# One mixture-of-experts phase: VectorE's side work spread one piece to a chunk, two router exponentials made from Tanh and squares, later down products

## The chip, the cores and the metric

One core of one Trainium2 chip runs the kernel. The metric is device time in microseconds (us) of one execution. The engines are named as in the profile: PE is TensorE, ACT is ScalarE, DVE is VectorE, POOL is GpSimd, SP is SyncE.

## What is computed

A small language-model tower over x, 8 sequences of 256 tokens: a stack of causal convolutions with a log-softmax, a linear attention, and a transformer block whose second half is the part of interest. With 2048 rows of 64 channels, 8 experts and top 2:

```
flat = rmsnorm(x, ln2_w)                       # 2048 x 64
probs = softmax(flat @ router_w.T)             # 2048 x 8
tp, ti = top_k(probs, 2);  tp = tp / (sum(tp) + 1e-09)
weights = sum over the two of tp * one_hot(ti)
for e in range(8):                             # hidden size 170
    hh = silu(flat @ w1[e].T) * (flat @ w3[e].T)
    out = out + weights[:, e:e+1] * (hh @ w2[e].T)
return x + out
```

## The kernel before

Each engine has its own program, written out by hand; the order of the work is the order in these programs, and semaphores join them. The change touches the last phase, the experts, and the router work that stands among them.

The 2048 rows are four pairs (n_ = 0 to 3) of 512 rows. For each pair the 8 experts are 11 chunks (i = 0 to 10): 8 chunks are the first 128 hidden units of an expert, and 3 chunks (the 1st, 5th and 9th in the order) are the remaining 42 units of three experts together. So there are 44 chunks, numbered u = 11 * n_ + i. What happens to chunk u:

- PE multiplies by w1 (two matmuls of 512 columns, a high and a low half of the weights) into one of two banks, then by w3 into one of two others (lines 1949 to 1959). The w1 product waits until ACT has done the silu of chunk u - 2, the w3 product until DVE has read chunk u - 2.
- ACT makes the silu of the w1 product (line 825), then the 16-bit cast, the high part, of chunk u - 1 (line 810).
- DVE multiplies the silu by the w3 product into a ring of 6 buffers (line 1362). This is called the product of chunk u below.
- POOL subtracts the high part to get the low part (line 414, `low_part`).
- When the parts of two experts are there, PE makes their down products (`down(n_, k, t_)`, k = 0 to 3 the two experts 2k and 2k + 1, t_ = 0 to 3 a block of 128 rows). `FILLED = (3, 6, 8, 11)` says how many chunks of the pair's low parts each k needs; `FREED` says which down products must be over before a slot of high and low parts is written again.
- DVE weighs the down products by the gates: `mix` (line 1290) for k = 0 and 2, `mix_add` (lines 1297 and 1299) for k = 1 and 3, which weighs and then adds to the k before. PE sums them in a bank (`sum_up`, with the identity as one operand), and `result` (line 1307) adds the rest.

Among the chunks stands other work, pinned to chunk numbers by `if u == ...` lines in each engine's loop:

- The norm of pairs 2 and 3: `rms_square` (lines 1178 to 1180, DVE), `third_root` (line 349, POOL, 1/sqrt by a power), `rms_rows` (line 1188, DVE), `third_split` (lines 343 and 344, POOL), `f_transposed` (line 1768, PE), `f_rows` (line 754, ACT). The transposed rows of pair 3 are first needed by chunk 33. `head_sum(B - 1)` (lines 396 to 398, POOL, after its chunk 10) makes the last rows of x2, which `rms_square(3)` reads.
- The router: `routed` (PE), `router_in` (lines 1206 and 1207, DVE), `router_exp` (line 759, ACT; pairs 0 and 1 before the loop, pairs 2 and 3 together ahead of chunk 24), and the top 2 and its gates on DVE: `ranks` (lines 1218 to 1221), `ranks_end` (1225, 1226) and `gates` (1231 to 1237), at the chunks of `GATE_STEPS`.

Each such piece comes in an engine's program after its own step of chunk u (on ACT before the silu of chunk u), and an engine does nothing out of order: a piece that waits holds up all that stands behind it.

Of the kernel before, what the change touches and what calls it, by code (L numbers as in the profile page):

```python
# [27 lines left out]
def tower(nc, x, tcn_w, tcn_b, out2_b, emb, in_b, attn_q, attn_e, qkv_w, wo_t, ln1, ln2, router,  # L28
# [8 lines left out]
    with ctx:  # L37
# [3 lines left out]
        def sem(name):  # L41
# [139 lines left out]
                 "rexp_ready", "gate_ready", "a_ps", "b_ps", "sil_ready", "hh_ready", "w2_ps", "mix_ready",  # L181
# [17 lines left out]
        GATE_STEPS = ((3, 4, 6), (14, 15, 16), (25, 26, 27), (30, 31, 34))  # L199
# [4 lines left out]
        sumP, recP = bank[7][:, 288:292], bank[7][:, 292:296]  # L204

# [67 lines left out]
        def _(pool):  # L273
# [263 lines left out]
            for u in range(PAIRS * CH):  # L537
                low_part(u)
                if u == 4:
                    third_root(2)  # L540
                if u == 7:
                    third_split(2)
# [4 lines left out]
                if u == 16:  # L547
                    third_split(3)
# [5 lines left out]
        def _(act):  # L554
# [206 lines left out]

            def last_pair_rows():
# [70 lines left out]
        def _(dve):  # L833
# [341 lines left out]
            def rms_square(p):  # L1175
                g4 = slice(4 * p, 4 * p + 4)
                dve.wait_ge(S["x2_ready"], 2 * p + 2)
                link(V_.tensor_tensor(sqr[:, p % 2, :, :], x2[:, g4, :], x2[:, g4, :], ALU.mult))
                link(V_.tensor_reduce(stat[:, 10, g4], sqr[:, p % 2, :, :], AX, ALU.add))
# [28 lines left out]

            def ranks(p):
# [5 lines left out]
                e_i = lg[:, p, :, :].unsqueeze(3).to_broadcast([P, 4, NE, NE])  # L1215
                e_j = lP.unsqueeze(2).to_broadcast([P, 4, NE, NE])
                low = lowidx[:, :, :].unsqueeze(1).to_broadcast([P, 4, NE, NE])
                link(V_.tensor_copy(lP, lg[:, p, :, :]))
                link(V_.tensor_tensor(gt[:, :, :, :], e_j, e_i, ALU.is_gt))
                link(V_.tensor_tensor(geP, e_j, e_i, ALU.is_ge))  # L1220
# [72 lines left out]
            def mix_add(n_, k):  # L1293
# [3 lines left out]
                link(V_.tensor_tensor(downs(b_, tt), downs(b_, tt), weights_of(n_, k, tt), ALU.mult))  # L1297
                dve.wait_ge(S["mix_ready"], 2 * n_ + k // 2 + 1)
# [55 lines left out]
            for u in range(PAIRS * CH):  # L1354
# [700 lines left out]
```

## Time and profile before

| what | us |
|---|---|
| median of the three runs | 244.01 |
| lowest and highest of them | 243.47, 332.02 |
| the profiled execution's own time | 243.33 |
| its span in the profile | 241.2 |
| the expert stretch, from PE's work between chunks 0 and 1 to DVE's last rows | 158.74 to 235.5 |

The profiled execution took 243.33 us, of which 241.2 are the span from the first to the last instruction and 2.1 lie around it. The trace is of this execution. All times below are from the start of the span.

### The profile page before, as it was taken

To read this page: it belongs to the slowest core of one execution; us is meant where nothing else is said; L and a number is where in the kernel's file an instruction comes from. 1 tells how busy PE (TensorE), PEld (TensorE's weight loads), DVE (VectorE), ACT (ScalarE), POOL (GpSimd) and SP (SyncE) were. 2 spreads that over 40 slices of the span, in tenths; PEclk is the share of its full clock that TensorE was granted. 3 is DMA by queue.
4 is the path that set the end of the run, shared out by engine and by line. 5 is a ranking of instruction groups with operands and counts; after the bars stand their busy time and mean duration, and the time that the engine had idled before them with its cause. 6 is when DMAs were issued, how large, how long until landed. Compare 5 with 4: busy or idle time off the path is not lost.

```text
span 241.2 us, 7322 instructions
## 1 busy us (share of the span) xinstructions
PE 205.2 (85%) x2836; PEld 133.9 (55%) x2836; DVE 175.4 (73%) x415; ACT 153.9 (64%) x279; POOL 145.3 (60%) x196
## 2 busy tenths in 40 slices
PE   7977788878898997886868989988799799898991
PEld 3643446345665665654756667744465465465671
DVE  4224665959785689888875869469869964999586
ACT  2378867277796777955546556576776579476670
POOL 6850000133687756682578886647989774776781
PEclk9999999999999999999999999999999999999999
DMA  1577300000000000000000000000000010010010
GB/s 35 126 167 167 85 16 3 0 3 3 3 1 3 3 3 3 5 0 3 0 3 0 3 3 0 4 0 4 0 4 0 3 23 3 0 24 0 3 26 22
DMA packets 8398, 4.52 MB, mean 19 GB/s; under 512 B 7557, under 2 KB 7853, under 8 KB 8365
## 3 DMA queue, kind: packets, MB, share of 16 engines
q1 hardware_dynamic: 8364, 4.06, 7.5%
q8 instruction: 23, 0.38, 0.6%
q14 instruction: 11, 0.08, 0.1%
HBM read 3.53 MB, written 0.52 MB: 17 GB/s over the span
## 4 chain that ended last, share of the span: by engine, by line
PE 45%; DVE 26%; ACT 11%; issue 9%; POOL 7%; DVEq 0%; POOLq 0%; ACTq 0%
PE bank L1401 42%; DVE shared L1362 3%; DVE nmx L1139 2%; ACT early L680 2%; ACT oT L665 2%; DVE L L1329 1%; POOL shared L414 1%; POOL stat L372 1%; ACT oTx L671 1%; DVE oT L1171 1%; ACT qT L825 1%; DVE early L872 1%; PE bank L1657 1%; DVE shared L979 1%; ACT early L566 1%
## 5 line engine op out<-in xcount | busy, mean ns | idle before, releaser
L1401 PE MATMUL bank<-early 64*64 64x256 f32 (+5 forms) x556 | 56.5, 352 | 9.6 <-DVE early L872 2.7
L414 POOL TENSOR_TENSOR shared<-shared 128x512 f16<-128x512 f32 x44 | 51.3, 1165 | 17.2 <-ACT shared L810 14.5
L1401 PEld LDWEIGHTS bank<-early 64*64 64x64 f32 (+3 forms) x556 | 30.5, 126 | 27.3 <-ACT early L559 5.2
L1362 DVE SCALAR_TENSOR_TENSOR shared<-bank,qT 128x512 f32<-128x512 f32 x44 | 29.7, 688 | 12.4 <-ACT qT L825 11.9
L810 ACT CAST shared<-shared 128x512 f16<-128x512 f32 x44 | 27.0, 614 | 12.1 <-DVE shared L1362 12.1
L825 ACT ACTIVATE qT<-bank 128x512 f32<-128x512 f32 x44 | 26.3, 597 | 10.5 <-PE bank L1401 10.3
L349 POOL TENSOR_TENSOR stat<-stat,neghalf 128x4 f32<-128x4 f32 x8 | 8.2, 1020 | 36.7 <-DVE stat L957 35.3
L1401 PE MATMUL bank<-onehot,w3h 128*128 128x512 f16 x88 | 26.3, 380 | 3.7 <-DVE shared L1362 3.5
L481 POOL TENSOR_TENSOR oTx<-oT,oTx 128x512 f16<-128x512 f32 x16 | 19.4, 1213 | 12.2 <-ACT oTx L671 12.2
L1401 PE MATMUL bank<-onehot,w1h 128*128 128x512 f16 x88 | 26.2, 380 | 0.3 <-ACT qT L825 0.3
L1401 PE MATMUL bank<-w2xh,shared 128*128 128x128 f16 (+1 forms) x240 | 22.4, 209 | 2.8 <-POOL shared L414 2.4
L1401 PE MATMUL bank<-w2h,shared 128*128 128x64 f16 x384 | 22.7, 193 | 0.0
L1401 PE MATMUL bank<-qT,shared 64*64 64x128 f32 (+1 forms) x320 | 18.5, 326 | 4.9 <-ACT oT L665 2.0
L1401 PEld LDWEIGHTS bank<-w2xh,shared 128*128 128x128 f16 x240 | 15.7, 98 | 10.2 <-POOL shared L414 4.6
L1139 DVE TENSOR_REDUCE nmx<-bank 128x2 f32<-128x512 f32 (+1 forms) x24 | 16.1, 688 | 7.1 <-PE bank L1401 6.8
L743 ACT ACTIVATE qT<-bank 128x512 f32<-128x512 f32 x24 | 14.3, 598 | 7.7 <-PE bank L1401 7.6
L872 DVE TENSOR_TENSOR early<-early 128x512 f32<-128x512 f32 x10 | 6.9, 693 | 16.4 <-ACT early L566 15.9
L1401 PEld LDWEIGHTS bank<-w2h,shared 128*128 128x128 f16 x384 | 18.3, 98 | 0.0
L1401 PEld LDWEIGHTS bank<-qT,shared 64*64 64x64 f32 x320 | 10.8, 132 | 12.1 <-issue 6.8
L1401 PEld LDWEIGHTS bank<-onehot,w3h 128*128 128x128 f16 x88 | 7.8, 97 | 16.3 <-DVE shared L1362 8.4
L665 ACT ACTIVATE oT<-bank 128x512 f32<-128x512 f32 x16 | 9.5, 596 | 10.7 <-PE bank L1401 10.5
L979 DVE TENSOR_TENSOR shared<-bank,trimul 128x512 f32<-128x512 f32 x16 | 11.0, 688 | 7.0 <-PE bank L1401 5.2
(228 smaller groups left out, 459.1 us busy)
## 6 DMA issues: line engine op xcount, KB each, us to landing
early<-in_tcn_w_dram SPq DMA_DIRECT2D x2, 320.0 KB, 4.4
w1s<-in_w1m_dram SPq DMA_DIRECT2D x2, 256.0 KB, 3.5
qT<-in_w3m_dram SPq DMA_DIRECT2D x2, 256.0 KB, 3.6
out_dram<-L SPq DMA_DIRECT2D x8, 64.0 KB, 1.7
qw<-in_attn_q_dram SPq DMA_DIRECT2D x4, 64.0 KB, 2.5
hTs<-in_w2m_dram SPq DMA_DIRECT2D x1, 256.0 KB
cos<-in_cos_t_dram SPq DMA_DIRECT2D x2, 96.0 KB, 2.3
sin<-in_sin_t_dram SPq DMA_DIRECT2D x2, 96.0 KB, 2.1
```

The source lines that it names most:

```text
L349: nc.gpsimd.tensor_tensor(stat[:, dst, g4], stat[:, src, g4], neghalf[:, 0:4], ALU.pow) \
L414: nc.gpsimd.tensor_tensor(hhx[:, i, 1, :], hh[:, u % RING, :], hhx[:, i, 0, :], ALU.subtract).then_inc(S["lo_ready"], 1)
L481: nc.gpsimd.tensor_tensor(oTx[:, g % 2, 1, :, :], oT[:, g % 2, :, :], oTx[:, g % 2, 0, :, :], ALU.subtract).then_inc(S["o_low"], 1)
L665: nc.scalar.mul(oT[:, g % 2, :, :].rearrange("p a (cc t) -> p cc a t", cc=2), banks[:, 6:8, 0:256].rearrange("p cc (a t) -> p cc a t", a=4 ...
L743: nc.scalar.activation(pT[:, b % 2, u, :], bank[5 + (3 * b + u) % 2][:, :], ACT.Exp).then_inc(S["exp2_ready"], 1)
L810: nc.scalar.copy(hhx[:, i, 0, :], hh[:, u % RING, :]).then_inc(S["hi_ready"], 1)
L825: nc.scalar.activation(sil[:, u % 2, :], bank[A_BANK[u % 2]][:, :], ACT.Silu, scale=1.0 / FFN_SCALE).then_inc(S["sil_ready"], 1)
L872: V_.tensor_tensor(x_, x_, hid2[:, 2 * s:2 * s + 2, :], ALU.add).then_inc(S["x_ready"], 1)
L979: V_.tensor_tensor(om[:, g % 2, :].rearrange("p (x j t) -> p x j t", x=2, t=64), banks[:, 4:6, 0:256].rearrange("p x (j t) -> p x j t", t=64),
L1139: V_.tensor_reduce(nmx[:, g, h0:h0 + nh], bank[4 - (3 * b + u) % 2][:, :].rearrange("p (n s) -> p n s", n=nh), AX, ALU.max, negate=True).t ...
L1362: V_.scalar_tensor_tensor(hh[:, u % RING, :], bank[B_BANK[u % 2]][:, :], HH_SCALE / FFN_SCALE, sil[:, u % 2, :], ALU.mult, ALU.mult).then_ ...
L1401: return nc.tensor.matmul(out_, l_, r_, start=a, stop=z, skip_group_check=skip)
```

## The change

Part 1 spreads DVE's work: `ranks` is cut into `ranks` and `ranks_even`, `mix_add` into `weigh_odd` and `add_odd`, `GATE_STEPS` has four steps, and nearly every piece stands at another chunk. Part 2 replaces the exponentials of pairs 2 and 3: with t = tanh(x/16) the exponential is the eighth power of (1 + t)/(1 - t), scaled alike, so ACT makes a Tanh, DVE the quotient (`eighth_root`), ACT three squares. Part 3 moves PE's down products k = 2 and 3 and the sums one or more chunks later. With these the steps of the norm of pairs 2 and 3 move on POOL, DVE, ACT and PE.

```diff
-        GATE_STEPS = ((3, 4, 6), (14, 15, 16), (25, 26, 27), (30, 31, 34))
+        GATE_STEPS = ((4, 5, 6, 7), (9, 14, 15, 18), (23, 25, 26, 29), (31, 34, 36, 37))
...
+        restP = bank[7][:, 296:328].rearrange("p (a e) -> p a e", a=4)
```

On POOL:

```diff
                 low_part(u)
+                if u == 1:
+                    third_root(2)
                 if u == 4:
-                    third_root(2)
-                if u == 7:
                     third_split(2)
                 if u == 10:
                     head_sum(B - 1)
                 if u == 13:
                     third_root(3)
-                if u == 16:
+                if u == 20:
                     third_split(3)
```

On ACT:

```diff
+            def router_tanh(p):
+                act.wait_ge(S["rexp_in"], p + 1)
+                nc.scalar.activation(lg[:, p, :, :], lg[:, p, :, :], ACT.Tanh, scale=1.0 / (16 * FFN_SCALE)) \
+                    .then_inc(S["tanh_ready"], 1)
+            def router_squares(p):
+                act.wait_ge(S["eighth_ready"], p - 1)
+                for i in range(3):
+                    r = nc.scalar.activation(lg[:, p, :, :], lg[:, p, :, :], ACT.Square)
+                    if i < 2:
+                        r.then_inc(S["squared"], 1)
+                        act.wait_ge(S["squared"], 2 * (p - 2) + i + 1)
+                r.then_inc(S["rexp_ready"], 1)
...
+                if u == 14:
+                    router_tanh(2)
                 if u == 21:
+                    router_squares(2)
+                if u == 23:
                     f_rows(3, SUM_BANK)
-                if u == 24:
-                    router_exp(2)
-                    router_exp(3)
+                if u == 26:
+                    router_tanh(3)
+                if u == 30:
+                    router_squares(3)
```

On DVE:

```diff
+            def eighth_root(p):
+                dve.wait_ge(S["tanh_ready"], p - 1)
+                l_ = lg[:, p, :, :]
+                link(V_.tensor_scalar(restP, l_, -1.0, 1.0, ALU.mult, ALU.add))
+                link(V_.reciprocal(restP, restP))
+                V_.scalar_tensor_tensor(l_, l_, 1.0, restP, ALU.add, ALU.mult).then_inc(S["eighth_ready"], 1)
...
-                if n_ and i == 1:
+                if n_ and i == 0:
+                    add_odd(n_ - 1, 1)
+                if n_ and i == 2:
                     mix(n_ - 1, 2, DOWN_BANK[0])
-                if n_ and i == 4:
-                    mix_add(n_ - 1, 3)
-                if n_ and i == 8:
+                if n_ and i == 5:
+                    weigh_odd(n_ - 1, 3)
+                if n_ and i == 6:
+                    add_odd(n_ - 1, 3)
+                if n_ and i == 9:
                     result(n_ - 1)
-                if i == 7:
+                if i == (8 if n_ < PAIRS - 1 else 7):
                     mix(n_, 0, DOWN_BANK[0])
                 if i == 10 and n_ < PAIRS - 1:
-                    mix_add(n_, 1)
-                if u == 7:
+                    weigh_odd(n_, 1)
+                if u == 3:
                     rms_rows(2)
                 if u == 12:
+                    rms_square(3)
+                if u == 13:
                     router_in(2)
-                    rms_square(3)
-                if u == 16:
+                if u == 19:
+                    eighth_root(2)
+                if u == 20:
                     rms_rows(3)
-                if u == 22:
+                if u == 24:
                     router_in(3)
+                if u == 28:
+                    eighth_root(3)
```

On PE:

```diff
-                if u == 20:
+                if u == 22:
                     f_transposed(3, SUM_BANK)
-                if u == 22:
+                if u == 24:
                     routed(3, SUM_BANK)
-                if n_ and i == 0:
-                    down(n_ - 1, 2, 2)
-                    down(n_ - 1, 2, 3)
-                if n_ and i == 2:
-                    down(n_ - 1, 3, 0)
-                    down(n_ - 1, 3, 1)
+                if n_ and i in (0, 1):
+                    down(n_ - 1, 2, 2 * i)
+                    down(n_ - 1, 2, 2 * i + 1)
+                if n_ and i in (3, 4):
+                    down(n_ - 1, 3, 2 * i - 6)
+                    down(n_ - 1, 3, 2 * i - 5)
+                if n_ and i == 5:
                     sum_up(n_ - 1, 0)
-                if n_ and i == 3:
-                    down(n_ - 1, 3, 2)
-                    down(n_ - 1, 3, 3)
+                if n_ and i == 8:
+                    sum_up(n_ - 1, 2)
...
                 if i == 6:
                     down(n_, 0, 2)
                     down(n_, 0, 3)
-                    if n_:
-                        sum_up(n_ - 1, 2)
...
-                if i == 10:
+                if i == 10 and n_ == PAIRS - 1:
                     down(n_, 2, 0)
                     down(n_, 2, 1)
```

`f_transposed(2)` and `routed(2)` stay at PE's chunks 10 and 12, `f_rows(2)` at ACT's chunk 11. `rms_square` now uses one half of a scratch tile whatever the pair, since the other half holds the ranks of pair 1 from chunk 9 on.

## Rows read from the trace of the kernel before

**Rows 1.** The page, part 1: busy time (share of the span) and instructions.

```profile
PE 205.2 (85%) x2836; PEld 133.9 (55%) x2836; DVE 175.4 (73%) x415; ACT 153.9 (64%) x279; POOL 145.3 (60%) x196
```

**Rows 2.** Windows: busy time of each engine in the expert stretch, columns in the first line.

```profile
core 0: us, PE busy (x) PEld busy (x) DVE busy (x) ACT busy (x) POOL busy (x), PEclk, DMA share, GB/s
158.74:235.50 76.76, 69.84 (x856) 43.64 (x856) 61.95 (x134) 53.02 (x96) 58.69 (x57) 1.00 0.03 7
```

**Rows 3.** Waits of TensorE, 159.5 to 233.8: engine line <- releaser: us in total, times, longest.

```profile
PE bank L1401 <- DVE shared L1362: 3.5, 5, 1.2
PE bank L1401 <- POOL shared L414: 1.9, 2, 1.2
PE bank L1768 <- POOL shl L344: 0.5, 1, 0.5
```

**Rows 4.** Timeline, PE: start, us, engine, line, operation, count, [idle before <-releaser].

```profile
165.50 0.34 PE L1401 MATMUL bank<-w2xh,shared 128*128 128x128 f16 x3
...
171.28 0.26 PE L1401 MATMUL bank<-w2xh,shared 128*128 128x64 f16 x3 [1.16 <-POOL shared L414]
...
175.03 0.40 PE L1768 MATMUL bank<-ident,shl 128*128 128x128 f16 x4 [0.45 <-POOL shl L344]
...
190.92 0.60 PE L1401 MATMUL bank<-onehot,w3h 128*128 128x512 f16 x2 [1.21 <-DVE shared L1362]
...
202.79 0.60 PE L1401 MATMUL bank<-onehot,w1h 128*128 128x512 f16 x2 [0.29 <-ACT qT L825]
...
205.82 0.34 PE L1401 MATMUL bank<-w2xh,shared 128*128 128x128 f16 x3 [0.69 <-POOL shared L414]
...
211.51 0.60 PE L1401 MATMUL bank<-onehot,w3h 128*128 128x512 f16 x2 [0.88 <-DVE shared L1362]
...
219.39 0.60 PE L1401 MATMUL bank<-onehot,w3h 128*128 128x512 f16 x2 [0.62 <-DVE shared L1362]
...
223.01 0.59 PE L1401 MATMUL bank<-onehot,w1h 128*128 128x512 f16 x2
```

**Rows 5.** Timeline, ACT, same columns.

```profile
199.19 1.28 ACT L759 ACT_TABLE_LOAD   x1
200.48 0.35 ACT L759 ACTIVATE lg<-lg 128x32 f32<-128x32 f32 x2
200.85 1.28 ACT L825 ACT_TABLE_LOAD   x1
...
223.64 0.60 ACT L825 ACTIVATE qT<-bank 128x512 f32<-128x512 f32 x1 [0.44 <-PE bank L1401]
224.13 0.61 ACT L810 CAST shared<-shared 128x512 f16<-128x512 f32 x1
```

**Rows 6.** Timeline, DVE, same columns.

```profile
171.59 1.15 DVE L1188 TENSOR_TENSOR s<-idx,stat 128x256 f32<-128x256 f32 x1
...
180.89 0.43 DVE L1178 TENSOR_TENSOR sqr<-idx 128x256 f32<-128x256 f32 x1 [0.52 <-POOL idx L398]
...
183.47 0.18 DVE L1218 COPY bank<-lg 128x32 f32<-128x32 f32 x1
...
188.54 0.41 DVE L1188 TENSOR_TENSOR s<-idx,stat 128x256 f32<-128x256 f32 x1
...
224.27 0.69 DVE L1362 SCALAR_TENSOR_TENSOR shared<-bank,qT 128x512 f32<-128x512 f32 x1 [0.86 <-ACT qT L825]
```

**Rows 7.** Timeline, POOL, same columns.

```profile
163.06 2.39 POOL L414 TENSOR_TENSOR shared<-shared 128x512 f16<-128x512 f32 x2 [0.46 <-ACT shared L810]
...
169.08 1.02 POOL L349 TENSOR_TENSOR stat<-stat,neghalf 128x4 f32<-128x4 f32 x1
...
173.82 0.40 POOL L343 CAST shl<-s 128x256 f16<-128x256 f32 x1
174.30 0.67 POOL L344 TENSOR_TENSOR shl<-s,shl 128x256 f16<-128x256 f32 x1
...
179.06 0.73 POOL L396 TENSOR_TENSOR oT<-oT 128x256 f32<-128x256 f32 x1
...
224.88 2.40 POOL L414 TENSOR_TENSOR shared<-shared 128x512 f16<-128x512 f32 x2 [0.39 <-ACT shared L810]
```

More of the change, by code:

```diff
@@ L1177, in rms_square @@
                 dve.wait_ge(S["x2_ready"], 2 * p + 2)
-                link(V_.tensor_tensor(sqr[:, p % 2, :, :], x2[:, g4, :], x2[:, g4, :], ALU.mult))
-                link(V_.tensor_reduce(stat[:, 10, g4], sqr[:, p % 2, :, :], AX, ALU.add))
+                link(V_.tensor_tensor(sqr[:, 0, :, :], x2[:, g4, :], x2[:, g4, :], ALU.mult))
+                link(V_.tensor_reduce(stat[:, 10, g4], sqr[:, 0, :, :], AX, ALU.add))
                 V_.tensor_scalar(stat[:, 7, g4], stat[:, 10, g4], 1.0 / C, 1e-6, ALU.mult, ALU.add) \
@@ L1214, in ranks, with ranks_even @@
                     dve.wait_ge(S["ym_ready"], TILES)
-                e_i = lg[:, p, :, :].unsqueeze(3).to_broadcast([P, 4, NE, NE])
-                e_j = lP.unsqueeze(2).to_broadcast([P, 4, NE, NE])
-                low = lowidx[:, :, :].unsqueeze(1).to_broadcast([P, 4, NE, NE])
+                e_j, e_i = both_ways(p)
                 link(V_.tensor_copy(lP, lg[:, p, :, :]))
                 link(V_.tensor_tensor(gt[:, :, :, :], e_j, e_i, ALU.is_gt))
+            def ranks_even(p):
+                e_j, e_i = both_ways(p)
+                low = lowidx[:, :, :].unsqueeze(1).to_broadcast([P, 4, NE, NE])
                 link(V_.tensor_tensor(geP, e_j, e_i, ALU.is_ge))
@@ L1291, in mix, with weigh_odd @@
                     .then_inc(S["mix_ready"], 1)
-            def mix_add(n_, k):
+            def weigh_odd(n_, k):
                 tt, b_ = slice(0, 4), DOWN_BANK[1]
@@ L1297, in mix_add, with add_odd @@
                 link(V_.tensor_tensor(downs(b_, tt), downs(b_, tt), weights_of(n_, k, tt), ALU.mult))
+            def add_odd(n_, k):
+                tt, b_ = slice(0, 4), DOWN_BANK[1]
                 dve.wait_ge(S["mix_ready"], 2 * n_ + k // 2 + 1)
@@ L1365, in _ @@
                     shares(B - 1)
-                if n_ and i == 1:
+                if n_ and i == 0:
+                    add_odd(n_ - 1, 1)
+                if n_ and i == 2:
                     mix(n_ - 1, 2, DOWN_BANK[0])
-                if n_ and i == 4:
-                    mix_add(n_ - 1, 3)
-                if n_ and i == 8:
+                if n_ and i == 5:
[3 more added lines that the diff above has]
+                if n_ and i == 9:
                     result(n_ - 1)
-                if i == 7:
+                if i == (8 if n_ < PAIRS - 1 else 7):
                     mix(n_, 0, DOWN_BANK[0])
                 if i == 10 and n_ < PAIRS - 1:
-                    mix_add(n_, 1)
-                if u == 7:
+                    weigh_odd(n_, 1)
+                if u == 3:
                     rms_rows(2)
                 if u == 12:
+                    rms_square(3)
+                if u == 13:
                     router_in(2)
-                    rms_square(3)
-                if u == 16:
+                if u == 19:
+                    eighth_root(2)
+                if u == 20:
                     rms_rows(3)
-                if u == 22:
+                if u == 24:
                     router_in(3)
-                for p_, (first, second, third) in enumerate(GATE_STEPS):
+                if u == 28:
+                    eighth_root(3)
+                for p_, (first, second, third, fourth) in enumerate(GATE_STEPS):
                     if u == first:
@@ L1388, in _ @@
                     if u == second:
+                        ranks_even(p_)
+                    if u == third:
                         ranks_end(p_)
-                    if u == third:
+                    if u == fourth:
                         gates(p_)
```

5 lines of the change are left out of this document (4 added, 1 removed).

## The prediction

> **What bounds the kernel now.** I read the page's busy line first, then the windows, the waits of PE, and at last the timeline of each engine, chunk by chunk. The page says that PE is busy 85% of the span and no other engine more than 73% [rows 1]. The change touches only the experts, so the windows come next: in the stretch from 158.74 to 235.50 (76.76 us) PE is busy for 69.84, DVE for 61.95, POOL for 58.69, ACT for 53.02, at the full clock [rows 2]. PE's work is thus the floor, and PE idles 6.9 us. The waits say for whom: DVE's product of a chunk 3.5 us, POOL's low parts 1.9, POOL's split of the normed rows 0.5 [rows 3].
>
> The idle time in brackets understates a stall. The product of w3 at 190.92 has 1.21 in brackets, but the matmuls ahead of it started at 189.12 and two of them take 0.43, so PE could have gone on at 189.55 and lost 1.37: the bracket and 0.16 more. Going through PE's timeline in this way I find 17 stalls in the stretch, 9.4 us in all. Seven are shown [rows 4]: down(0, 1) at 171.28 (1.32), the transposes of pair 2 at 175.03 (0.61), w3 of chunk 19 at 190.92 (1.37), w1 of chunk 26 at 202.79 (0.45), down(2, 0) at 205.82 (0.85), w3 of chunk 30 at 211.51 (1.04), w3 of chunk 35 at 219.39 (0.78). Ten others sum to 3.0, the first before w3 of chunk 5 (0.68), which the change leaves. PE's own work is not changed: 0.87 a chunk, 0.69 half a down product (two t_), 0.96 a sum, and only its order moves. The change is worth what it takes from these 9.4 us, less the stalls that it makes.
>
> **How far each step of a chunk trails.** A chunk with nothing beside it: chunk 37 has w1 at 223.01 [rows 4], silu at 223.64 and the cast of chunk 36 at 224.13 [rows 5], product at 224.27 [rows 6], low part of chunk 36 at 224.88 [rows 7]. So silu is 0.63 after w1, the product 0.63 after silu, the cast 0.5 after the next chunk's silu, the low part 0.75 after its cast, and it takes 1.2. A product frees DVE after 0.60 and PE's w3 of two chunks on after 0.74.
>
> **Part 1, DVE spread (with the sums later).** Nothing of DVE's work goes, it is cut: ranks was 4 instructions (1.60, the first at 183.47 [rows 6]) and becomes 0.67 and 0.93; the rest are mix 0.60, weigh 0.73, add 0.60, gates 1.30, ranks_end 0.92. In the old order three such pieces stand between products 16 and 17 and hold back w3 of chunk 19; in the new one the longest is gates alone, 1.30. I walked all 44 chunks with the durations above. From chunk 17 on PE's stalls at chunks 18, 19, 29, 30 and 35 go: 0.12 + 1.37 + 0.13 + 1.04 + 0.78 = 3.44. Nothing new appears there by the walk; for instance w3 of chunk 30 needs product 28, which is done 0.8 before it. DVE has 61.95 of work to PE's 67.4 (76.76 less the stalls), so bunching was the cause and not the sum.
>
> **Part 2, Tanh and squares.** Before chunk 24 ACT loads the table of Exp (1.28), does two exponentials (0.35) and loads that of Silu again (1.28): 2.9 us [rows 5]. PE pays for it at chunks 26 and 27 and down(2, 0): 0.45 + 0.30 + 0.14 + 0.85 = 1.74 [rows 4]. No trace row shows Tanh or Square, so they are bounded: from 0.22 each (a small exponential) with no load, to a load of 1.28 at each Tanh and at the silu behind it. I take no load, since casts and copies run under any table here and the two ends differ in kind; the other end is a rival. The added DVE work is three small instructions (0.65) twice, and ACT's three linked squares are 0.75 twice. ACT has some 0.45 free in each chunk, and PE's distance covers a silu late by 0.8; except at one place, below. Gain: 1.74.
>
> The trace shows 1.28 for each load and the exponential starting 0.01 after it [rows 5]. The Trainium skill (ScalarE: Activation LUTs, "What ACT_TABLE_LOAD costs") gives the same 1283 ns, and adds a drain of 1.38 to each switch. The rows show no such drain here; with it, part 2 would save 2.8 more of ACT's time, PE's share of which would not be in the stalls that I read.
>
> **Part 3 and the moved norm steps.** Four places.
> (a) Pair 2's root now runs on POOL behind low part 1. It takes 1.0 (the one at 169.08 [rows 7]), and low part 2 stood at 164.25 right behind low part 1 (two low parts from 163.06 on, 1.2 each [rows 7]). down(0, 0) waits for exactly this low part: it started at 165.50 [rows 4] and now starts at 166.5. Part of that was lost anyway (0.48 at w3 of chunk 6). The split moves ahead of low part 5 too (1.15). So down(0, 1), at 171.28 before, comes at 171.8: +0.5.
> (b) rms_rows(2), now between products 3 and 4, has both inputs in the same memory as POOL's low parts. One such instruction took 1.15 while POOL worked, the other 0.41 while POOL stood [rows 6]. I take 1.15: low part 2 starts as it does. At 0.41, the 0.5 of (a) becomes 0.1. The Trainium skill (SBUF — State Buffer, the part on the two sides of the memory) says that such an instruction with two inputs there and POOL's exclude each other for a whole instruction. By that rule it is 1.15 here, and 0.41 if they merely shared.
> (c) Pair 2's transposes no longer wait, with the split three chunks earlier: 0.61 gone. The small stalls at the sum (0.33) and at down(1, 0) (0.27) go from their places: 1.21 together. But rms_square(3) moves to right behind product 12, ahead of mix and router_in. It needs head_sum(7), which follows low part 10 and takes 1.8 (at 179.06, and rms_square at 180.89 [rows 6, 7]). Before, DVE had 1.0 of other work first and still waited 0.52. In my walk product 12 ends at 178.7, the sum at 180.4, and product 13 starts at 181.8; w3 of chunk 15 waits 1.2 for it. Behind product 13 come mix and router_in, and Tanh on ACT, ahead of silu 14, waits for router_in: silu 14 at 183.7, which costs w1 and w3 of chunk 16 another 0.7 and 0.3. New: 2.2.
> (d) Pair 3's transposes are behind chunk 22 on PE, and their split is behind low part 20 on POOL, two chunks earlier instead of four. Product 20 is at 193.8. On ACT the squares of pair 2 stand before silu 21, so the cast of chunk 20 is at 195.1; low part 20 at 195.85; the split (0.40 and 0.67, in all 1.2 [rows 7]) ends at 198.25. PE is done with chunk 22 at 195.45, as no down product follows chunk 21 any more. It waits 2.85; the small stall of 0.29 that these transposes had goes. Bounds: with every step as in chunk 37 low part 20 ends 0.6 after PE has done chunk 22, and with the split PE waits 1.8, less 0.7 if PE itself is late: 1.1; with DVE or ACT a further piece behind, 4.0.
> At the end, mix(3, 0), result(2) and last_odd bunch before product 43: 0.15.
>
> **The sum.** Gone: 3.44 + 1.74 + 1.21 + 0.29 = 6.68. New: 0.5 + 2.2 + 2.85 + 0.15 = 5.7. Net 1.0 faster; the last chunks of the walk itself give 0.7, and I take 0.9. The profiled execution took 243.33 (2.1 of it outside the span), so 242.4. The median of the three runs is 244.01, but the two ordinary ones are 243.47 and 244.01, so the profiled one is as good a base as these. Without the stall of (d) the same change would be worth nearly 4 us.
>
> **The rivals.**
> A, the stall of (d) is short: PE runs later than in my walk, or ACT's squares don't come between. PE then waits 1.1 or less, and (c) costs 1.2 instead of 2.2 if ACT isn't held: 242.4 - 1.75 - 1.0 = 239.7. For it: PE's lag in a real run soaks up part of any fixed chain. Against: in the undisturbed chunk 37 the distance already falls short by 1.8.
> B, Tanh needs another table than Silu. Then there are four loads in two places, not two in one, and each place costs as the old one did, 1.74: 242.4 + 3.5 = 245.9. For it: the rows show every change of function costing a load (Exp, Silu). Against: nothing in the trace has a Tanh. 
> C, the other side: the wait of the transposes of pair 3 grows. Its place is w3 of chunk 22 to the transposes, its cause low part 20 behind products 19 and 20, which come behind gates(1), mix, and eighth_root. Each us that product 20 is later is a us on PE, with nothing behind to take it up. From a wait of 3.8 on the change loses; at 5.0 it is 244.5. For it: gates, mix and eighth_root stand behind three products in a row, and ACT's squares wait for the last. Against: PE would be late with chunk 22 too, since w3 of chunk 22 waits for product 20.
> D, the spread frees nothing because PE's stalls move on to the next tight product (DVE has only 5 us less work than PE): half of the 3.44 stays, 244.1.
>
> **Chances.** Forecast (241 to 243.3) 0.47, A 0.22, B 0.07, C 0.12, D 0.12. From 239.2 to 245.6 lie all but parts of A, B and C. Measurements of this kernel tell about 2% (4.9 us) from no change: below 238.5 lies only the best part of A, 0.05; above 248.2 only B together with C, 0.03; within, 0.92.
>
> **What would show it.** In the profile after: no table load after the first Silu; no stall at w3 of chunks 19, 30, 35; PE idle before the transposes of pair 3 by over 2, released by POOL's L344 step; DVE idle over 1 before rms_square(3), released by the head sum; down(0, 0) at 166.5. The prediction is wrong if pair 3's transposes wait less than 1, or if a table load stands at each Tanh.

## The result, and the profile after

| | before | after |
|---|---|---|
| median of 20 executions each | 244.05 | 243.21 |
| lowest | 243.38 | 241.24 |
| profiled execution, its span | 243.33, 241.2 | 241.91, 240.2 |
| expert stretch (PE's start between chunks 0 and 1 to DVE's last rows) | 76.83 | 75.07 |

The ratio is 0.9923 with a 95% interval of 0.9898 to 0.9949: 1.2 to 2.5 us faster. It leaves out slow executions, the five of the changed kernel above 245.5 among them, which the medians in the table keep. The forecast was 0.9 us faster, 242.4. The executions of the changed kernel spread from 241.2 to 246.0 with the granted clock of TensorE: six with a mean of 0.995 or 0.996 have a median of 241.47, four with 0.989 or 0.990 one of 242.76, five with 0.981 to 0.983 one of 243.67, and five with 0.975 one of 245.80. An experiment below takes this up.

The stretch starts 0.71 later in this trace than in the one before (159.45 against 158.74); 0.49 of that is there by 33 us, where the two kernels are the same, and the traces of all the runs below start it between 158.77 and 160.74. So stretches are compared, from their own start. Before, the stretch ends at 235.57. One part of the gain is not in the span at all: around it lay 2.1 us before and lie 1.7 now.

The page's busy line of the changed kernel, against [rows 1], says nearly nothing:

```profile
PE 203.6 (85%) x2836; PEld 134.9 (56%) x2836; DVE 176.5 (73%) x421; ACT 152.9 (64%) x283; POOL 145.0 (60%) x196
```

Nor does the busy time by engine in the expert stretch (columns in the first line), against [rows 2]: less of PE, 0.8 more of DVE, 1.1 less of ACT, in 1.76 us less.

```profile
core 0: us, PE busy (x) PEld busy (x) DVE busy (x) ACT busy (x) POOL busy (x), PEclk, DMA share, GB/s
159.45:234.52 75.07, 67.95 (x856) 44.37 (x856) 62.75 (x141) 51.88 (x100) 58.84 (x57) 1.00 0.03 7
```

What changed is who holds up PE. Its waits in the changed kernel (total, times, longest) have other names than [rows 3]: the split of the normed rows, 0.5 before, is first, and DVE's product has fallen from 3.5 in 5 waits to 1.7 in 2.

```profile
PE bank L1819 <- POOL shl L345: 2.8, 1, 2.8
PE bank L1452 <- POOL shared L415: 1.9, 2, 1.0
PE bank L1452 <- DVE shared L1402: 1.7, 2, 1.2
...
PE bank L1452 <- ACT qT L847: 0.4, 1, 0.4
```

PE's timeline shows the places; after the w3 of chunk 16 there is one stall up to the last chunk, where the kernel before had eleven, large and small [rows 4].

```profile
167.20 0.34 PE L1452 MATMUL bank<-w2xh,shared 128*128 128x128 f16 x3 [1.00 <-POOL shared L415]
...
172.37 0.26 PE L1452 MATMUL bank<-w2xh,shared 128*128 128x64 f16 x3 [0.86 <-POOL shared L415]
...
175.51 0.39 PE L1819 MATMUL bank<-ident,shl 128*128 128x128 f16 x4
...
183.20 0.61 PE L1452 MATMUL bank<-onehot,w3h 128*128 128x512 f16 x2 [1.17 <-DVE shared L1402]
...
184.87 0.60 PE L1452 MATMUL bank<-onehot,w1h 128*128 128x512 f16 x2 [0.38 <-ACT qT L847]
...
186.04 1.03 PE L1452 MATMUL bank<-qst,identf 128*128 128x256 f32 x4
186.90 0.33 PE L1452 MATMUL bank<-w2xh,shared 128*128 128x128 f16 x3
...
198.68 0.40 PE L1819 MATMUL bank<-ident,shl 128*128 128x128 f16 x4 [2.80 <-POOL shl L345]
```

Read with the rule of the prediction (the bracket and 0.16): down(0, 0) waits 1.17 at 167.20, down(0, 1) 1.03 at 172.37; the transposes of pair 2 at 175.51 don't wait; w3 of chunk 15 waits 1.33, w1 and w3 of chunk 16 wait 0.53 and 0.29; the transposes of pair 3 wait 2.97. The stalls from 164 to the last chunk sum to 8.2, before it was 9.4. Behind the last chunk two waits stand in both kernels alike (0.26 and 0.57 in brackets). The pair at 186.04 and 186.90 is for later: a sum that takes 0.86, where one before took 0.94:

```profile
187.19 1.11 PE L1401 MATMUL bank<-qst,identf 128*128 128x256 f32 x4
188.13 0.59 PE L1401 MATMUL bank<-onehot,w1h 128*128 128x512 f16 x2
```

ACT's timeline has no table load behind the first silu; the one in [rows 5] is gone. Tanh takes 0.23 and the three squares 0.75:

```profile
184.10 0.23 ACT L766 ACTIVATE lg<-lg 128x32 f32<-128x32 f32 x1 [3.33 <-DVE lg L1229]
184.24 0.58 ACT L847 ACTIVATE qT<-bank 128x512 f32<-128x512 f32 x1
...
194.39 0.75 ACT L773 ACTIVATE lg<-lg 128x32 f32<-128x32 f32 x3 [0.23 <-DVE lg L1237]
195.05 0.58 ACT L847 ACTIVATE qT<-bank 128x512 f32<-128x512 f32 x1
```

DVE's timeline has the two places at which it waits. rms_rows(2) idles 0.52 for the root and then takes 1.37 beside POOL's low parts; rms_square(3) idles 1.75 for the last rows of x2 [rows 6 for both before]; product 20 stands at 194.28:

```profile
166.05 1.37 DVE L1210 TENSOR_TENSOR s<-idx,stat 128x256 f32<-128x256 f32 x1 [0.52 <-POOL stat L350]
...
181.09 0.42 DVE L1200 TENSOR_TENSOR sqr<-idx 128x256 f32<-128x256 f32 x1 [1.75 <-POOL idx L399]
...
194.28 0.69 DVE L1402 SCALAR_TENSOR_TENSOR shared<-bank,qT 128x512 f32<-128x512 f32 x1
```

And POOL's timeline has the root ahead of low part 2, and the split of pair 3 behind low part 20, which is the third line from below [rows 7 for the same steps before]:

```profile
165.00 1.02 POOL L350 TENSOR_TENSOR stat<-stat,neghalf 128x4 f32<-128x4 f32 x1
165.99 2.46 POOL L415 TENSOR_TENSOR shared<-shared 128x512 f16<-128x512 f32 x2
...
196.26 1.15 POOL L415 TENSOR_TENSOR shared<-shared 128x512 f16<-128x512 f32 x1 [0.81 <-DVE s L1210]
197.48 0.40 POOL L344 CAST shl<-s 128x256 f16<-128x256 f32 x1
197.96 0.67 POOL L345 TENSOR_TENSOR shl<-s,shl 128x256 f16<-128x256 f32 x1
```

The releaser named at low part 20 (196.26), `rms_rows(3)`, was done at 195.73; what low part 20 needs is the cast of chunk 20, which ran from 195.52 to 196.13.

### The profile page after: what moved, and what is told of

Its sections match the earlier page's. It is cut to its first block, busy times and chain, and to the rows that moved or that the text cites. A ratio compares the mean times of both kernels' runs of the same rounds, so it can differ in the third digit from the quotient of the medians.

```text
span 240.2 us, 7337 instructions
## 1 busy us (share of the span) xinstructions
PE 203.6 (85%) x2836; PEld 134.9 (56%) x2836; DVE 176.5 (73%) x421; ACT 152.9 (64%) x283; POOL 145.0 (60%) x196
## 4 chain that ended last, share of the span: by engine, by line
PE 49%; DVE 21%; ACT 10%; POOL 9%; issue 9%; DVEq 0%; POOLq 0%; ACTq 0%
PE bank L1452 47%; POOL shared L415 2%; DVE nmx L1161 2%; ACT early L681 2%; ACT oT L666 2%; DVE L L1369 1%; POOL stat L373 1%; ACT oTx L672 1%; DVE early L894 1%; PE bank L1708 1%; DVE shared L1001 1%; ACT early L567 1%; DVE shared L1402 1%; DVE nmr L1172 1%; DVE oT L1193 1%
## 5 line engine op out<-in xcount | busy, mean ns | idle before, releaser
L1402 DVE SCALAR_TENSOR_TENSOR shared<-bank,qT 128x512 f32<-128x512 f32 x44 | 30.3, 689 | 8.3 <-ACT qT L847 7.4
L1452 PEld LDWEIGHTS bank<-onehot,w3h 128*128 128x128 f16 x88 | 8.3, 98 | 13.2 <-DVE shared L1402 4.0
```

The source lines that it names most:

```text
L1402: V_.scalar_tensor_tensor(hh[:, u % RING, :], bank[B_BANK[u % 2]][:, :], HH_SCALE / FFN_SCALE, sil[:, u % 2, :], ALU.mult, ALU.mult).then_ ...
L1452: return nc.tensor.matmul(out_, l_, r_, start=a, stop=z, skip_group_check=skip)
```

## The experiments

The theory: PE's work is the floor of the stretch, each stall of PE is worth its length. By the two lists of stalls the change removed 7.4 us of them and made 6.3 (forecast 6.7 and 5.6, without the 0.15 at the end). The rival: stalls hand work on, and what is freed at one place is lost at the next. Each figure of a stretch below is from PE's start between chunks 0 and 1 to the start of DVE's last rows, in the run's trace; a ratio is against the kernel before on the same chip.

**The long stall at the transposes of pair 3** (split3_early).

```diff
# POOL and VectorE of the changed kernel
-                if u == 20:
+                if u == 17:
                     third_split(3)
...
-                if u == 20:
+                if u == 17:
                     rms_rows(3)
```

> The changed kernel with the normed rows and the split of pair 3 at chunk 17 instead of 20 on VectorE and GpSimd, TensorE as it is. Theory (every stall of TensorE is worth its length): the wait of 2.97 us before the transposes of pair 3 goes to 0, nothing else moves, 2.5 to 3.0 us faster than the changed kernel, a span near 237.4. Rival (the work saved up during the stall comes back): TensorE stalls at chunks 22 to 28 for VectorE or GpSimd's low parts instead, under 1 us gained. On the clock: if the long stall is what lowers the granted clock in some executions of the changed kernel (means of 0.975 to 0.996), the means here all lie above 0.99; if it is not the cause, the spread of 241 to 246 stays.

Measured: a stretch of 72.90, 2.17 less than the changed kernel's; 239.99 us median of 4, ratio 0.9822 (0.9765 to 0.988). The transposes don't wait. A new stall stands just ahead of them, at w3 of chunk 22:

```profile
196.61 0.60 PE L1452 MATMUL bank<-onehot,w3h 128*128 128x512 f16 x2 [0.65 <-DVE shared L1402]
```

It waits for DVE's product 20, and costs 0.81: 2.97 - 0.81 = 2.16. So the gain lies between the theory's 2.5 to 3.0 and the rival's 1.0: the theory holds less this one hand-over, which the idle time had covered. On the clock, the means of the four executions are 1.0, 0.993, 0.989 and 0.983, so they don't all lie above 0.99 as they should if the long stall alone lowered it.

**The wait of rms_square(3)** (square3_late).

```diff
-                if u == 12:
-                    rms_square(3)
                 if u == 13:
                     router_in(2)
+                    rms_square(3)
```

> The changed kernel with rms_square(3) behind product 13 and router_in(2) instead of behind product 12. Theory: VectorE no longer stands 1.75 us for the last rows of x2 with router_in and Tanh behind it, so the stalls at w3 of chunk 15 and w1 and w3 of chunk 16 (1.33 + 0.53 + 0.30) go; VectorE still waits some 0.3 to 0.5 at the new place, of which TensorE feels nothing or little: 1.5 to 2.2 us faster than the changed kernel. Rival: the wait only moves a chunk on and w3 of chunk 16 or 17 stalls for a similar time, under 0.7 gained; and what is gained here comes back at the transposes of pair 3, whose wait grows if TensorE comes there earlier while GpSimd does not (product 20 hangs on VectorE's own chain), so the net is under 0.7.

Measured: the stalls at chunks 15 and 16 fell from 2.15 in all to 0.84 (w3 of chunk 16). PE reached the transposes of pair 3 1.34 earlier from the start of the stretch and waited 2.97 for them as before: GpSimd's split moved with VectorE's products, so the hand-over that the rival wanted did not occur. The theory's 1.5 to 2.2 was a little high. The stretch itself is 75.36 in this trace, as the clock was at half for 3.4 us behind the long stall; the ratio is 0.9923 (0.9893 to 0.9954), the same as that of the changed kernel, so the 1.34 is seen in the trace alone.

**The root of pair 2** (root2_first).

```diff
+            third_root(2)
             for u in range(PAIRS * CH):
                 low_part(u)
-                if u == 1:
-                    third_root(2)
```

> The changed kernel with the root of pair 2 on GpSimd before low part 0 instead of behind low part 1. Theory: low part 2 starts 1.0 us earlier, down(0, 0) no longer waits 1.18 and down(0, 1) comes some 0.5 to 1.0 earlier; but the transposes of pair 3 hang on VectorE's chain, so 0.4 to 1.0 us faster than the changed kernel. Rival: all of it is given back at down(0, 1) or at x2's last rows (low part 10 comes with the casts, not with the roots), 0 to 0.3.

Measured: a stretch of 74.11, 0.96 less. down(0, 0) waits 0.18 instead of 1.17, and nothing of it is given back later, though down(0, 1) still waits 1.06. The theory's upper end; the rival falls. Again it is the trace that shows it: the ratio is 0.9921 (0.9881 to 0.9961).

**The three together** (all_three).

> The changed kernel with the three edits of split3_early, square3_late and root2_first together. Alone they shortened the expert stretch of the changed kernel by 2.16, 1.34 and 0.95 us. Theory (each removes a different stall and TensorE is the floor): they add, 4.4 us off the stretch of 75.07, a time near 236.9 in an execution at full clock. Rival (the stalls hand work on to each other): the new stall of 0.81 at w3 of chunk 22 grows, 3 us or less off.

Measured: a stretch of 70.17, 4.90 less than the changed kernel's and 6.66 less than before's. The three alone sum to 2.17 + 1.34 + 0.96 = 4.47, and here the stall at w3 of chunk 22 has shrunk to 0.36. They add up and help each other. 237.10 us median of 4, ratio 0.9706 (0.9659 to 0.9753): faster than both kernels, and it leaves 3.3 us of stalls from w3 of chunk 5 to the last chunk.

**Tanh alone, on the kernel before** (before_tanh, before_tanh2). Added to it: router_tanh, eighth_root and router_squares as in the change, in place of `router_exp(2)` and `router_exp(3)`; the two kernels differ in where the quotients and squares stand.

```diff
# before_tanh, ACT: Tanh at 14 and 24, squares at 20 and 28; DVE: quotients at 18 and 25
# before_tanh2, ACT: Tanh at 14 and 24, squares at 22 and 30; DVE: quotients at 20 and 28
```

> Part 2 of the change alone on the kernel before: Tanh of pair 2 ahead of silu 14, of pair 3 ahead of silu 24, quotients behind products 18 and 25, squares ahead of silus 20 and 28; both exponentials ahead of chunk 24 and their two table loads gone. Theory: 1.74 us faster than before, the stalls at chunks 26, 27 and down(2, 0). Rival: the work of VectorE (0.65 twice) and ScalarE (0.75 twice) falls on stretches where VectorE is already the one that is late (products 17 and 28), 0 to 0.8 faster.

> before_tanh with the quotients at two chunks at which VectorE has less beside the product (20 and 28 instead of 18 and 25) and the squares two chunks behind each (22 and 30). In before_tanh the 1.74 us of stalls at the table loads went and 1.4 came back (at the transposes of pair 3 0.66 more, at w3 of chunk 28 0.56, at a sum 0.19). Theory (only the place of the added work cost this): these stay away, the stretch is 1.2 to 1.7 shorter than before. Rival (the kernel before has no free place on VectorE): 0.2 to 0.6 shorter as in before_tanh.

Measured: stretches of 76.50 and 75.96 against 76.83, so 0.33 and 0.87 less; ratios 0.9939 (0.9911 to 0.9967) and 0.9956 (0.9918 to 0.9994). No load of a table in either. The ratios say more than the stretches, for two reasons. In these kernels, too, 1.7 us lie around the span instead of 2.1 (the part on Tanh undone takes this up), and the clock of the kernel before fell in more executions than that of before_tanh. Between executions with a mean clock of 0.999 or more the medians are 243.66 for the kernel before and 243.06 for before_tanh. In before_tanh the stalls behind the loads are gone and these stand in their place, the transposes of pair 3 (0.29 before, 0.94 now) and w3 of chunk 28:

```profile
193.92 0.38 PE L1802 MATMUL bank<-ident,shl 128*128 128x128 f16 x4 [0.78 <-DVE L L1337]
...
206.45 0.61 PE L1435 MATMUL bank<-onehot,w3h 128*128 128x512 f16 x2 [0.40 <-DVE shared L1392]
```

In before_tanh2 both of these are gone, but w3 of chunks 33 and 35 and the first half of down(2, 2) wait 0.8 more than they did. The theory for the second (1.2 to 1.7) was too high and the rival (0.2 to 0.6) too low: place matters, and in DVE's old order there was no wholly free one.

**Tanh undone with the rest kept** (all_three_exp).

```diff
                 if u == 21:
-                    router_squares(2)
+                    router_exp(2)
...
                 if u == 30:
-                    router_squares(3)
+                    router_exp(3)
```

The two `router_tanh` and the two `eighth_root` go as well.

> all_three with the exponentials of pairs 2 and 3 by Exp at the places of the squares (ahead of silu 21 and silu 30), without Tanh and without the quotients on VectorE: part 2 of the change undone with the rest kept. Theory: each place has two table loads, 2.57 us of ScalarE, of which TensorE feels 1.0 to 1.7, as at chunks 26 to 28 of the kernel before; 2.0 to 3.4 us slower than all_three. Rival: with VectorE's work spread there is cover for the loads, as there is for the squares; under 1 us slower.

Measured: a stretch of 72.54, 2.37 more than all_three; 239.98 us median, ratio 0.9819 (0.9767 to 0.9871), against 237.10. The theory. PE's stalls at the two places:

```profile
195.05 0.60 PE L1442 MATMUL bank<-onehot,w1h 128*128 128x512 f16 x2 [1.02 <-ACT qT L842]
...
210.26 0.60 PE L1442 MATMUL bank<-onehot,w1h 128*128 128x512 f16 x2 [0.22 <-ACT qT L842]
```

The first is 1.19 and 0.28 behind it, the second 0.39 with 0.34 and 0.32 behind. So Tanh is worth 2.4 us of the stretch in the new order and 0.3 to 0.9 in the old one. The two are not the same comparison: here two separate exponentials with four table loads stand against Tanh, in the kernel before one place with two loads. What the joint exponentials of the kernel before would cost in the new order was not run, so how much of the difference between 2.4 and 0.9 is the spread and how much the two further loads stays open.

The medians differ by 2.9, more than the 2.4 of the stretch. Around the span (time less span) lie 2.06 to 2.11 us in all four executions of all_three_exp and 2.03 to 2.14 in all 59 of the kernel before, but 1.66 to 1.78 in every execution of all kernels with Tanh except all_three_bunched (1.81 to 1.86). So the exchange of Exp for Tanh and squares is worth some 0.35 us more, outside the span. Why was not tried.

**The old order of the down products** (all_three_downs_old): all_three with PE's `down` and `sum_up` lines of the kernel before.

> all_three with the down products and sums on TensorE in the order of the kernel before (part 3 undone, the transposes of pair 3 left at chunk 22). Theory (the later order is needed by the later adds): sum_up(n - 1, 2) behind chunk 6 waits for the add that VectorE now does behind product 6, some 1.2 us in each of three pairs; 3 to 4 us slower than all_three. Rival: the order on TensorE is of no matter, since the work is the same; under 1 us slower.

Measured: a stretch of 78.15, 7.98 more than all_three, and 245.56 us: slower than the kernel before (ratio 1.0034, 1.0005 to 1.0064). The new stalls stand before five of the six sums, 8.05 us in all:

```profile
181.13 1.13 PE L1450 MATMUL bank<-qst,identf 128*128 128x256 f32 x4 [1.22 <-DVE lg L1228]
...
189.16 1.13 PE L1450 MATMUL bank<-qst,identf 128*128 128x256 f32 x4 [1.39 <-DVE qst L1338]
...
202.22 1.13 PE L1450 MATMUL bank<-qst,identf 128*128 128x256 f32 x4 [1.44 <-DVE lg L1228]
...
210.25 1.13 PE L1450 MATMUL bank<-qst,identf 128*128 128x256 f32 x4 [1.39 <-DVE qst L1338]
...
229.12 1.13 PE L1450 MATMUL bank<-qst,identf 128*128 128x256 f32 x4 [1.79 <-DVE qst L1338]
```

The three with DVE's L1338, `add_odd`, are those expected (1.55, 1.55 and 1.95). I had missed the other two, 1.38 and 1.60: the first sum of pairs 0 and 1 waits for `router_in(2)` and `(3)`, because it overwrites what these read, and DVE now does them a chunk or two later. A down product behind chunk 21 waits 0.55 more, and the two stalls of all_three at w3 of chunks 16 and 22 (1.19) are gone. So with DVE's later adds the later order of PE is needed. Part 3 without part 1 was not run; it has one gain of its own, 0.1 in each sum, of which more in the next part.

**DVE's pieces joined again** (all_three_bunched).

```diff
-        GATE_STEPS = ((4, 5, 6, 7), (9, 14, 15, 18), (23, 25, 26, 29), (31, 34, 36, 37))
+        GATE_STEPS = ((4, 4, 6, 7), (9, 9, 15, 18), (23, 23, 26, 29), (31, 31, 36, 37))
...
-                if n_ and i == 0:
-                    add_odd(n_ - 1, 1)
...
                 if i == 10 and n_ < PAIRS - 1:
                     weigh_odd(n_, 1)
+                    add_odd(n_, 1)
```

and the same for `weigh_odd(n_ - 1, 3)`.

> all_three with VectorE's halves together again: ranks_even right behind ranks (chunks 4, 9, 23, 31), and add_odd right behind weigh_odd; the rest as it is. It is part 1 undone in its cuts. Theory (the longest piece between two products is what stalls TensorE): pieces of 1.33 and 1.6 us are no longer than gates with 1.3 and meet TensorE with its slack of 0.8 to 1.2 us, so three to six stalls of 0.2 to 0.8 appear, 1 to 3 us slower than all_three. Rival (only the sum of VectorE's work over some chunks counts, the cuts themselves are worth little): within 0.5 us of all_three.

Measured: a stretch of 70.78, only 0.61 more; 238.55 us median, ratio 0.9755 (0.971 to 0.98), and 237.34 against 236.72 between the executions with a mean clock of 0.998 or more (one against two, on two chips). The largest stalls are two that all_three has as well:

```profile
171.99 0.26 PE L1448 MATMUL bank<-w2xh,shared 128*128 128x64 f16 x3 [0.62 <-POOL shared L415]
...
184.33 0.61 PE L1448 MATMUL bank<-onehot,w3h 128*128 128x512 f16 x2 [0.90 <-DVE shared L1401]
```

They are 0.78 at down(0, 1) (1.06 in all_three) and 1.07 at w3 of chunk 16 (0.83), and new in kind are only 0.43 at w3 of chunk 7, 0.37 at that of chunk 35 and two under 0.2. Nearer to the rival: the cuts are worth 0.6, and pieces of 1.6 hurt little where they stand here. That it counts more which pieces fall together fits before_tanh and before_tanh2, which differ in places alone and by 0.54; but the old places of part 1 were not put back into the new order, so for part 1 itself this is argued and not shown.

**The rest of the stalls** (all_three_more).

```diff
-                if u == 4:
+                if u == 5:
                     third_split(2)
...
-                if u == 13:
+                if u == 14:
                     third_root(3)
...
-        GATE_STEPS = ((4, 5, 6, 7), (9, 14, 15, 18), ...
+        GATE_STEPS = ((4, 5, 6, 7), (9, 12, 15, 18), ...
...
                     router_in(2)
+                if u == 14:
                     rms_square(3)
```

> all_three with the split of pair 2 on GpSimd behind low part 5 instead of 4, and rms_square(3) behind product 14 (its root one chunk later on GpSimd) with ranks_even of pair 1 at chunk 12, which has nothing beside the product. Theory: the stalls of all_three at down(0, 1) (1.06) and at w3 of chunk 16 (0.82) go, 1.5 to 1.9 us faster, near 235.0 at full clock. Rival: low part 5 was not held by the split but came late itself, and w3 of chunk 22 (0.36 now) or the transposes of pair 3 take up what is gained, 0 to 0.8.

Measured: a stretch of 69.89, 0.28 less; 237.19 us median, ratio 0.9703 (0.9661 to 0.9745), no different from all_three. Both stalls were cut: down(0, 1) waits no longer, and w3 of chunks 10 and 11 wait 0.30 and 0.10 instead; chunk 16 waits 0.17 and 0.28 instead of 0.83. But w3 of chunk 22 rose from 0.36 to 0.84:

```profile
193.25 0.61 PE L1451 MATMUL bank<-onehot,w3h 128*128 128x512 f16 x2 [0.68 <-DVE shared L1401]
```

Here the rival is right in its size, and in part in its mechanism: w3 of chunk 22 took half a us of what was gained. What holds PE next is probably DVE between chunks 13 and 22, where it has the norm, the router and the gates of pair 1 beside the products; that was not tested.

**The clock behind the long stall** (after_again, after_filled). after_again is the changed kernel. after_filled adds, ahead of the transposes of pair 3:

```diff
+                if p == 3:
+                    pe.wait_ge(S["rexp_in"], 3)
+                    pe.wait_ge(S["fin_ready"], 2)
+                    for _i in range(12):
+                        mm(bank[b_][:, :], ident16[:, :], w1h[:, 0, 0:4, :].rearrange("p j c -> p (j c)"), True, True)
                 pe.wait_ge(S["fsplit_ready"], p + 1)
```

> The changed kernel once more, beside after_filled and on the same chip, for the granted clock of each execution. In the trace of square3_late the clock stood at 0.5 for 3.4 us right behind the stall of 2.97 us at the transposes of pair 3; the executions of the changed kernel had means of 0.996, 0.989, 0.982 and 0.975. Theory: that long stall costs one such piece in part of the executions, so means of 0.989 and less appear in a good part of them. Rival: the means are those of the kernel before on the same chip, which has them too without this stall.

> The changed kernel with 12 matmuls of 512 columns (2.6 us, results never read) on TensorE in the place of the stall before the transposes of pair 3; everything real runs when it did. Theory (the idle 2.97 us are what lets the clock fall behind it): at full clock the time of the changed kernel within 0.3 us, but its mean clocks higher, with one step of 0.007 fewer in many executions, a median 0.5 to 1.5 us below after_again. Rival (the falls have nothing to do with that stall): the same clocks and the same median.

Windows of 2 us around the stall, after_again (the column PEclk is the granted clock):

```profile
core 0: us, PE busy (x) PEld busy (x) DVE busy (x) ACT busy (x) POOL busy (x), PEclk, DMA share, GB/s
196.00:198.00 2.00, 1.17 (x6) 0.32 (x4) 2.00 (x5) 1.97 (x6) 1.19 (x2) 1.00 0.15 35
198.00:200.00 2.00, 0.02 (x1) 0.03 (x2) 1.54 (x3) 0.43 (x1) 1.86 (x4) 1.00 0.16 35
200.00:202.00 2.00, 2.00 (x24) 1.72 (x25) 0.00 (x0) 0.58 (x1) 1.03 (x1) 0.54 0.00 0
202.00:204.00 2.00, 2.00 (x20) 1.18 (x19) 0.49 (x1) 1.10 (x2) 0.17 (x1) 0.60 0.00 0
```

and the same windows of after_filled:

```profile
196.00:198.00 2.00, 2.00 (x11) 0.92 (x10) 1.97 (x4) 1.14 (x3) 1.59 (x3) 1.00 0.31 70
198.00:200.00 2.00, 1.78 (x27) 1.12 (x25) 0.28 (x1) 0.59 (x1) 1.75 (x2) 1.00 0.00 0
200.00:202.00 2.00, 2.00 (x25) 1.27 (x24) 1.09 (x3) 1.31 (x3) 0.52 (x1) 1.00 0.00 0
202.00:204.00 2.00, 2.00 (x33) 1.38 (x32) 1.61 (x5) 1.96 (x4) 1.61 (x2) 1.00 0.04 8
```

In after_again PE is idle in the second window, and in the third and fourth the granted clock is 0.54 and 0.60: half speed, 1.2 GHz, for 3.4 us. The stretch is 76.71 long against 75.07 in the first trace of the same kernel: 1.64 us for it. Filled, the clock stays at 1.00 and the stretch is 75.08, since real work ran when it did. Four traces have the unfilled stall of 2.97: in two of them (after_again, square3_late) such a piece begins 0.2 to 0.4 after PE starts again, in the other two (the first of the changed kernel, root2_first) there is none in the stretch. None of the ten traces without that stall has one in its stretch. Of 12 executions of after_again 7 have a mean clock of 0.982 or less, of 6 of after_filled none (0.986 to 0.996), and the medians are 243.78 and 241.88, at spreads of 241.36 to 245.76 and 241.32 to 242.95. If the filling did nothing, all 7 such executions would fall among the 12 by chance in about 1 case in 40. The theory holds as far as these few executions tell, with 1.9 instead of 0.5 to 1.5. The changed kernel itself is as before, with a ratio of 0.994 (0.9903 to 0.9976). The stall doesn't explain all: both traces also have a mean of 0.83 from 120 to 130, ahead of the experts, and 14 of 17 executions of the kernel before on this chip have means of 0.982 to 0.993 without any long stall in the experts.

## Why the prediction was right, and where it was off

- What bounds: PE, held up by single waits. Right; every experiment moved the stretch by nearly the stalls that it took or made, but for the clock in two traces and for the length of the sums (below).
- Part 1, 3.44 gone from chunk 17 on: right. None of the five stalls is there, and none came in their place. No run undid this part by itself, apart from its cuts (0.6).
- Part 2, 1.74 gone, no table load: right here, and rival B falls. What it is worth in the stretch hangs on what stands around it and on how many loads it saves (0.3 and 0.9 in the old order against two loads, 2.4 in the new one against four), which the prediction did not say. It also took some 0.35 from the time around the span, which the prediction kept at 2.1.
- Part 3 and the norm, (a) and (b): down(0, 0) at 166.5 was the forecast, and it came at 167.20, in a trace that is 0.71 later: 166.49. down(0, 1) at 171.66 by the same count, 171.8 forecast. rms_rows(2) took 1.37, not 1.15, and no stall came of it. The 1.15 of [rows 6] is not a fixed price: in all 14 traces every rms_rows of pairs 2 and 3 that started beside a low part (25 of 28) took 0.42 to 1.37 and ended 0.28 to 0.30 after that low part's end, whenever it had started. As the Trainium skill has it (SBUF — State Buffer, "SBUF: two separate sides"), such an instruction is locked out for the whole length of a running GpSimd instruction, and the trace agrees: 1.37 beside a low part against the 0.41 of [rows 6] with POOL idle.
- (c): 2.2 forecast for chunks 15 and 16, 2.15 measured; DVE's wait for x2 1.7 forecast, 1.75 measured.
- (d): 2.85 forecast, 2.97 measured, by the chain named: product 20, the squares, the cast, low part 20, the split. Rivals A and C fall.
- The 0.15 at the end did not come: DVE's product 43 starts 1.27 after w1 of chunk 43, and 1.26 before.
- The sum: the terms gave 1.0 and the forecast was 0.9; the stretch lost 1.76. The term that was mis-sized is PE's own work, "0.96 a sum" with "only its order moves". A sum is four fp32 matmuls. In the kernel before all six take 0.94 to 0.97, in the changed kernel 0.86 or 0.87, 0.55 us together. Taken one by one, the matmuls are 0.22 apart, except that in the longer sums the second comes 0.30 to 0.32 after the first. It is what stands ahead of the sum that differs, not what stands behind: the long ones start behind the small down products or after a wait, the short ones directly behind a w3 product. In all_three_downs_old, with down products ahead of them again, all six take 0.95 to 0.97. And in all_three_more this sum has down products behind it as in the changed kernel, but starts 0.10 late, and takes 0.96:

```profile
187.35 0.59 PE L1451 MATMUL bank<-onehot,w3h 128*128 128x512 f16 x2
187.89 1.13 PE L1451 MATMUL bank<-qst,identf 128*128 128x256 f32 x4
188.85 0.25 PE L1451 MATMUL bank<-w2xh,shared 128*128 128x64 f16 x3
```

- The rest of the difference: 0.15 at the end, 0.12 at down(0, 1), 0.05 at (c), less 0.12 at (d). With the sums this gives 1.75 of the 1.76.
- From the stretch to the time: 1.76 less the 0.71 by which it starts later, and 0.37 from around the span, are the 1.42 of the profiled executions. The lowest executions differ by 2.14, about the 1.76 and 0.37 together.
- Luck: that the medians differ by 0.84, so close to the forecast of 0.9, is not the sum coming out. The lowest executions gained 2.1; the median of the changed kernel then lies 2.0 above its lowest, with the lower means of the clock in the list under the result, and that of the kernel before only 0.7. What the forecast did not see is that the long stall can cost more than its length. after_again and after_filled bear out that it is a cause of the lower clock, but not that it is the only one.

Rival D, that freed stalls move on, was given 0.12 and did not hold for the change. It held in part at the next steps, in split3_early (0.81 of 2.97) and in all_three_more.

## What to carry to other kernels

Where an in-order engine is the floor and is held up by single waits, list its stalls, walk the new order by hand from the distances of one undisturbed piece, and count for each moved step the chain up to whoever waits for it. A step that is moved behind another engine's piece needs as many pieces of distance as its chain is long: here the chain over the split to the transposes cost TensorE 0.6 us at a distance of 3 chunks (pair 2 before), 3 us at 2 and nothing at 5 and 6. Spreading, later consumers and a cheaper function hang together: undone one at a time in the order of all_three, the cuts of VectorE's work cost 0.6 us of the stretch, the later down products 8.0 and Tanh 2.4. And a forecast that comes out may still owe part of that to terms that cancel: read the parts as well as the total.

## What the runs showed of the hardware

- A stall of TensorE of 2.97 us was followed in two of four traces by 3.4 us at half the clock (1.2 GHz), which cost 1.64 us. With twelve matmuls whose results nobody reads in the stall, the clock stayed full there, and the median of 6 executions was 1.9 us below that of 12 without them.
- A sum of four fp32 matmuls of 256 columns takes 0.86 or 0.87 directly behind a 512-column product, and 0.94 to 0.97 behind small 16-bit down products or after a wait; the difference lies between its first and its second matmul. Why was not tried.
- Tanh (0.23) and Square (0.25 each in a chain) ran between silus without a table load, where Exp brought two of 1.28.
- A VectorE instruction with two inputs in the same memory as a running GpSimd low part ended 0.28 to 0.30 after that low part, whenever it had started (25 of 25), and took 0.42 to 1.37; with GpSimd idle it took 0.41.
- With Exp in place of Tanh and squares the time around the span was 2.1 us instead of 1.7.
